# Attention probabilities left undivided: the outputs are multiplied by turned inverse sums

## The chip, the cores and the metric

The kernel runs on one core of a Trainium2 chip, as one launch. The metric is the device time of a launch in microseconds, smaller is better; it comes as the median of several runs, with their extremes. A profile is one more execution, recorded by the hardware profiler.

## The reference

Input x is 64 sequences of 128 tokens with 256 features, the context 64 x 128 x 192. All in float32:

```
lat  = layernorm(x)                          # outer layernorm, then the attention's own with gain
q    = ln(lat) @ Wq.T                        # 4 heads of 64
k, v = [ln(ctx) @ Wkv.T ; ln(lat) @ Wlkv.T]  # 128 context + 128 latent keys
attn = softmax(mask(rmsnorm(q) * 64**-0.5 @ rmsnorm(k).T))
x1   = x + (attn @ v) @ Wo.T + bo
n1   = layernorm(x1)
out  = x1 + routed(n1) + shared(n1)          # 32 experts, 4 a token, in 4 groups of which 2 count;
                                             # and a shared gated FFN of 256
```

The part that matters here is the softmax: exp(s - max) divided by its sum over 256 keys, then multiplied with v.

## The kernel before

There are three stages. The attention stage takes 32 units of two sequences each (j = 0 and 1), one `step(s)` per unit on every engine; the routing of earlier units runs inside the same steps. Then come 288 tiles of the expert FFN, then the shared FFN and the sums. The change touches the attention stage alone.

Each engine runs its own list of instructions in order, written out by hand in its `step`; semaphores tie the lists together. A step s of the attention stage works on several units at once: scores and softmax of s, projections of a = s+1, layernorm turns of s+2, routing of s-2 (cc) and s-3 (r).

TensorE's order in a step (PE `step`, L931): scores j=0 and 1 (L813, with the mask added by L818), turns and logits of routing (L742, L866, L881 to L885), projections of the next unit (L757, L767, L770, again L757), `turn_probs` j=0 (eight 128x128 transposes, L827), `project_v` (L778), `turn_c` (L729), `mix_values` j=0 (sixteen matmuls, L840), `turn_x` (L720), `turn_probs` j=1, `out_proj` j=0 (L852), `turn_k` j=0 (L791, L792), `mix_values` j=1, `turn_k` j=1, `turn_q` (L800), `out_proj` j=1, and then the scores of the next step. Matmuls of 64 rows of the array (L813, L818, L770) or 64 columns (L840) stand between matmuls of all 128 by 128.

ScalarE's order (L1209): rows and layernorms, `exps` j=0 (L1160, which also leaves the sums of the exponentials in den), `weigh_probs` j=0 (L1168: four instructions that multiply the probabilities of a head by its inverse sum), `projected_q` (L1128, L1132), `exps` j=1, the copies of the projections (L1139, L1143, L1145, L1128, L1132), `probs_copy` j=0 (L1175, the turned probabilities from PSUM), the copies of the values (L1152), `weigh_probs` j=1, `o_copy` j=0 (L1182, mixed values from PSUM to oT), `inputs_x` (L1112), `probs_copy` j=1, `inputs_c` (L1120), `k_copy` (L1200), `o_copy` j=1, `k_copy`, `q_copy` (L1206).

VectorE's order (L1648): `maxima` j=0 (L1460), ranks and assignment of routing with the residual (L1473) and statistics (L1402) between, `invert_sums` j=0 (L1466: a reciprocal of 128x4), `maxima` j=1, more routing, `top_scores`, `invert_sums` j=1, two `square_sums` (L1418), `norms` (L1423 to L1448, a chain of small dependent instructions with weights of slots, L1589, between), two `scale_heads` (L1454), slots (L1596), `best_groups` and `best_experts` (L1491 to L1516) with input statistics between, `choose_experts` (L1524 to L1528). In the last step, that of unit 31, `square_sums` and `scale_heads` are gone, and `positions(s-2)` of TensorE stands behind `mix_values` j=1.

GpSimdE issues the scatters of routed rows (L556), each held back by a semaphore of TensorE's progress.

Of the kernel before, what the change touches and what calls it, by code (L numbers as in the profile page):

```python
# [17 lines left out]
P = 128  # L18
NB, D, DC = 64, 256, 192
H, DH = 4, 64  # L20
# [66 lines left out]
def build(nc, x, ctx, mask, gains, w_in_lat, w_in_ctx, wo, bo,  # L87
# [8 lines left out]
    with ExitStack() as c:  # L96
# [45 lines left out]
        probsT = part(2, 2, H * P)  # L142
        oT = part(D)
        vv = part(4 * 2, H, DH)

# [27 lines left out]
        nmax = sb("nmax", [P, 2, H])  # L173
        den, rden = sb("den", [P, 2, H]), sb("rden", [P, 2, H])

# [63 lines left out]
        s_full, m_done, exp_done = sem("s_full"), sem("m_done"), sem("exp_done")  # L239
        den_done, rden_done = sem("den_done"), sem("rden_done")  # L240
        spread = [sem("spread0"), sem("spread1")]
        pt_full, pt_ev = sem("pt_full"), sem("pt_ev")
        pv_full, ot_ev = sem("pv_full"), sem("ot_ev")
        y_full, y_done = sem("y_full"), sem("y_done")
# [465 lines left out]
        def _(pe):  # L710
# [111 lines left out]
            def turn_probs(u, j):  # L822
# [6 lines left out]
                m.then_inc(pt_full, 1)  # L829

            def mix_values(u, j):
                b = 2 * u.n + j
                pe.wait_ge(pt_ev, b + 1)
                pe.wait_ge(pc_free, 2 * u.n + 2)
                ge(pe, ot_ev, b)
                for ch in range(2):
                    for key in range(2):
                        for r in range(2):
                            g, h = 2 * r + ch, 2 * ch + r
                            m = pe.matmul(psO[r * DH:(r + 1) * DH, ch * P:(ch + 1) * P],  # L840
                                          vv[:, 4 * u.par + 2 * j + key, h, :], probsT[:, j, key, g * P:(g + 1) * P],
                                          start=key == 0, stop=key == 1)
                m.then_inc(pv_full, 1)
# [87 lines left out]
            def step(s):  # L931
# [12 lines left out]
                if a.exists():  # L944
                    project_q(a, 0)
                    project_kv(a)
                    project_q(a, 1)
                turn_probs(s, 0)
                if a.exists():
                    project_v(a, 0)  # L950
                    project_v(a, 1)
# [5 lines left out]
                turn_probs(s, 1)  # L957
                out_proj(s, 0)
                if a.exists():
                    turn_k(a, 0)  # L960
# [121 lines left out]
        def _(act):  # L1082
# [72 lines left out]
            def exps(u, j):  # L1155
                b = 2 * u.n + j
                act.wait_ge(m_done, b + 1)
                ge(act, pt_full, b - 1)
                for g in range(H):
                    a = act.activation(probs[:, j, g, :], score_banks[j][:, g // 2, g % 2], ACT.Exp,  # L1160
                                       bias=nmax[:, j, g:g + 1], accum_out=den[:, j, g:g + 1])
                a.then_inc(den_done, 1)

            def weigh_probs(u, j):
                b = 2 * u.n + j
                act.wait_ge(rden_done, b + 1)
                for g in range(H):
                    a = act.activation(probs[:, j, g, :], probs[:, j, g, :], ACT.Copy, scale=rden[:, j, g:g + 1])  # L1168
                a.then_inc(exp_done, 1)
# [7 lines left out]

            def o_copy(u, j):
                b = 2 * u.n + j
                act.wait_ge(pv_full, b + 1)  # L1180
                ge(act, y_full, b)
                act.activation(oT, psO[:, 0:D], ACT.Copy).then_inc(ot_ev, 1)  # L1182

# [25 lines left out]
            def step(s):  # L1209
# [9 lines left out]
                if cc.exists():  # L1219
                    logit_exp(cc)  # L1220
                weigh_probs(s, 0)
                if a.exists():
                    projected_q(a, 0)
                exps(s, 1)
                if a.exists():
                    projected_kv(a, 0)
                    projected_kv(a, 1)
                    projected_q(a, 1)
                probs_copy(s, 0)
                if a.exists():  # L1230
                    values_copy(a, 0)
                    values_copy(a, 1)
                weigh_probs(s, 1)
                o_copy(s, 0)
                if (s + 2).exists():
                    inputs_x(s + 2)
                probs_copy(s, 1)
                if (s + 2).exists():
                    inputs_c(s + 2)
                if a.exists():  # L1240
                    k_copy(a, 0)
                o_copy(s, 1)
                if a.exists():
# [120 lines left out]
        def _(dve):  # L1364
# [98 lines left out]
            def invert_sums(u, j):  # L1463
                b = 2 * u.n + j
                dve.wait_ge(den_done, b + 1)
                dve.reciprocal(rden[:, j, :], den[:, j, :]).then_inc(rden_done, 1)  # L1466

# [180 lines left out]
            def step(s):  # L1648
# [30 lines left out]

                def between_choices(n):  # L1680
                    if ahead.exists() and G_LINKS < n <= G_LINKS + 4:
                        input_part(ahead, n - G_LINKS - 1)
# [8 lines left out]
                invert_sums(s, 0)  # L1691
                maxima(s, 1)
                if r.exists():
                    assign_rest(r, between_moves)
# [7 lines left out]
                if a.exists():  # L1702
                    square_sums(a, 0)
                    square_sums(a, 1)
                norms(run, between_roots if a.exists() else None)
                if a.exists():
                    scale_heads(a, 0)
# [7 lines left out]
                if not cc.exists() or not a.exists():  # L1715
                    residual(s, 0)
                    x1_statistics(s, 0)
                if not cc.exists():
                    if ahead.exists():
                        input_statistics(ahead)  # L1720
# [248 lines left out]
```

## Time and profile before

| | us |
|---|---|
| median of 3 runs | 1344.24 (1341.73 to 1345.44) |
| profiled execution | 1343.46 |
| its span | 1341.5 |
| PE matmul busy | 1298.0 (97%) |
| ScalarE busy | 1011.6 (75%) |
| VectorE busy | 972.0 (72%) |
| GpSimdE busy | 643.4 (48%) |
| L1168, `weigh_probs`, 256 instructions | 109.1, mean 503 ns |

The span is what the instruction records cover; the profiled execution's time is 2 us more, for what lies around it. The attention stage fills the first half of the span, up to about 700 us; its steps repeat with a period of 20.58 us (the load for L813 begins at 319.50 and at 340.08 us).

### The profile page before, as it was taken

What the parts mean: (1) busy time and instruction counts of PE and PEld (TensorE: products, weight loads), DVE (VectorE), ACT (ScalarE), POOL (GpSimd) and SP (SyncE); (2) the same over time, 40 slices, a digit from 0 to 9 for tenths busy, and PEclk for the clock granted to TensorE, in tenths of its full rate; (3) what the DMA queues carried; (4) which work ended last, traced back from release to release, by engine and by line L of the source; (5) the groups of instructions that cost most, each with busy time, mean ns of one, the idle gap of its engine ahead of it and who ended that gap; (6) DMA issues with size and microseconds to landing.
All of it is one profiled execution on the core that took longest, in us unless ns stands there. A gap on an engine that the chain in (4) does not pass through costs nothing.

```text
span 1341.5 us, 32944 instructions
## 1 busy us (share of the span) xinstructions
PE 1298.0 (97%) x8718; PEld 1043.2 (78%) x8718; DVE 972.0 (72%) x4498; ACT 1011.6 (75%) x2730; POOL 643.4 (48%) x724
## 2 busy tenths in 40 slices
PE   6999999999999999999979899999999999999997
PEld 4566676676676766766658799999999999988886
DVE  4578898888988988888887455555555555548887
ACT  4899999999999999999851566766776676653332
POOL 1113555555555555555455366666666666640000
PEclk8999999999999999999989899999999999999999
DMA  8234645535545445454487655555655555438896
GB/s 278 84 133 136 205 162 176 192 131 187 176 138 190 161 153 195 136 179 162 168 304 246 194 169 172 172 172 168 178 169 174 169 173 166 132 114 313 304 319 218
DMA packets 147714, 247.14 MB, mean 184 GB/s; under 512 B 24139, under 2 KB 110413, under 8 KB 146896
## 3 DMA queue, kind: packets, MB, share of 16 engines
q1 hardware_dynamic: 121472, 177.63, 41.3%
q0 software_dynamic: 26064, 67.42, 14.5%
q8 instruction: 77, 1.26, 0.4%
q14 instruction: 101, 0.83, 0.2%
HBM read 104.68 MB, written 119.96 MB: 167 GB/s over the span
## 4 chain that ended last, share of the span: by engine, by line
PE 63%; ACT 21%; DVE 9%; issue 5%; DMA 2%; SPq 0%; POOL 0%; ACTq 0%; DVEq 0%
PE psT L1033 10%; PE ps L1033 9%; PE psS L1043 9%; ACT arena L1168 6%; PE ps L916 6%; PE ps L1024 5%; PE ps L852 4%; ACT arena L1160 4%; PE psS L927 3%; PE psT L827 3%; PE psS L813 3%; PE psO L840 2%; ACT arena L1128 2%; ACT arena L1132 2%; ACT arena L1175 2%
## 5 line engine op out<-in xcount | busy, mean ns | idle before, releaser
L701 POOL DMA_INDIRECT expert_out<-pay,dest x287 | 282.1, 983 | 175.1 <-DVE dest L1878 157.4
L556 POOL DMA_INDIRECT lists<-pay,slot x168 | 174.3, 1037 | 187.7 <-PE psT L827 39.6
L1043 PE MATMUL psS<-arena,history 128*128 x574 | 171.8, 381 | 0.3 <-DVE history L1865 0.3
L1033 PEld LDWEIGHTS ps<-pad,hist_j 128*128 128x128 f32 x1152 | 152.1, 193 | 9.5 <-ACT pad L1315 2.1
L1033 PEld LDWEIGHTS psT<-pad 128*128 128x128 f32 x1144 | 151.0, 192 | 7.3
L1033 PE MATMUL ps<-pad,hist_j 128*128 128x128 f32 x1152 | 152.8, 276 | 1.9 <-ACT pad L1315 1.9
L1033 PE MATMUL psT<-pad 128*128 128x128 f32 x1144 | 151.6, 276 | 0.0
L1872 DVE TENSOR_SCALAR pay<-psS,dest 128x256 f32<-128x256 f32 x287 | 138.9, 484 | 1.6 <-PE psS L1043 1.5
L757 PE MATMUL ps<-arena 128*128 128x512 f32 x256 | 128.3, 624 | 2.6 <-ACT arena L1120 2.0
L556 POOL DMA_INDIRECT lists<-arena,slot x88 | 91.0, 1034 | 79.4 <-PE psT L827 20.6
L1168 ACT ACTIVATE arena<-arena,rden 128x256 f32<-128x256 f32 x256 | 109.1, 503 | 15.2 <-DVE rden L1466 15.1
L1865 DVE TENSOR_TENSOR history<-history,psT 128x128 f32<-128x128 f32 x143 | 41.2, 288 | 102.4 <-ACT history L1326 102.4
L1865 DVE TENSOR_TENSOR history<-history,ps 128x128 f32<-128x128 f32 x144 | 41.5, 288 | 101.2 <-ACT history L1326 101.2
L1024 PE MATMUL ps<-ident,pay 128*128 128x128 f32 x574 | 110.0, 274 | 3.1 <-DMA arena<-in_gate_up 3.0
L1315 ACT ACTIVATE pad<-ps 128x256 f32<-128x256 f32 x287 | 107.7, 375 | 0.0
L1320 ACT ACTIVATE hist_j<-arena 128x512 f32 x144 | 89.6, 622 | 9.4 <-issue 7.6
L1326 ACT ACTIVATE history<-ps 128x128 f32<-128x128 f32 x144 | 39.9, 277 | 70.3 <-PE ps L1033 70.3
L757 PEld LDWEIGHTS ps<-arena 128*128 128x128 f32 x256 | 44.2, 193 | 59.2 <-issue 59.2
L1320 ACT ACTIVATE pad<-arena 128x512 f32 x143 | 88.8, 621 | 0.0
L1326 ACT ACTIVATE history<-psT 128x128 f32<-128x128 f32 x143 | 39.7, 278 | 65.0 <-PE psT L1033 65.0
L1043 PEld LDWEIGHTS psS<-arena,history 128*128 128x128 f32 x574 | 86.9, 192 | 0.7 <-issue 0.7
L1418 DVE TENSOR_REDUCE va<-arena 128x12 f32<-128x768 f32 x64 | 61.0, 953 | 34.2 <-ACT arena L1128 29.1
(238 smaller groups left out, 3284.1 us busy)
## 6 DMA issues: line engine op xcount, KB each, us to landing
lists<-pad SPq DMA_DIRECT2D x72, 516.0 KB, 5.2
pay<-lists SPq DMA_DIRECT2D x287, 129.0 KB, 2.2
arena<-expert_out SPq DMA_DIRECT2D x32, 1024.0 KB, 7.1
pay<-pay SPq DMA_DIRECT2D x42, 384.0 KB, 3.6
x<-in_x SPq DMA_DIRECT2D x32, 256.0 KB, 4.7
out<-arena SPq DMA_DIRECT2D x31, 256.0 KB, 5.8
arena<-arena SPq DMA_DIRECT2D x20, 384.0 KB, 3.4
arena<-in_ctx SPq DMA_DIRECT2D x32, 192.0 KB, 4.6
```

The costliest lines, as they stand in the source:

```text
L556: pool.indirect_dma_start(lists, bass.IndirectOffsetOnAxis(ap=slots(u)[:, j, k:k + 1], axis=0), paid(u)[:, j, k, :], None).then_inc(scat[3 ...
L701: pool.indirect_dma_start(expert_out, bass.IndirectOffsetOnAxis(ap=dest[:, t % DESTS, 1:2], axis=0), yy[n], None, bounds_check=T * TOPK - ...
L757: m = pe.matmul(ps[0][:, :], lnT[:, k, tok], w_lat[:, k, 0:2 * D], start=k == 0, stop=k == 1)
L916: m = pe.matmul(up_banks[u % 2][mm][:, which * D:(which + 1) * D], w[:, k, mm * P:(mm + 1) * P], n1T_of(u)[:, k, :], start=k == 0, stop=k ...
L1024: m = pe.transpose(ps[n % 2][:, k * P:(k + 1) * P], xs[n][:, k * P:(k + 1) * P], ident[:, :])
L1033: m = pe.matmul(ps[2 + n % 2][:, which * P:(which + 1) * P], w_now[1 - n % 2][:, k, which * I:(which + 1) * I], xsT[:, n % 2, k * P:(k + 1 ...
L1043: pe.matmul(dbank[n % 2][:, 0:D], hh[:, n % 4, :], w_dn[:, at(e, 1), :].rearrange("p a n -> p (a n)"), start=True, stop=True)\
L1168: a = act.activation(probs[:, j, g, :], probs[:, j, g, :], ACT.Copy, scale=rden[:, j, g:g + 1])
L1315: act.activation(xsT[:, n % 2, :], ps[n % 2][:, 0:D], ACT.Copy).then_inc(xst_ev, 1)
L1320: act.activation(w_now[1 - n % 2], w_gu[:, at(e, 1)].rearrange("p a k n -> p (a k) n"), ACT.Copy)\
L1865: dve.tensor_tensor(hh[:, n % 4, :], sg[:, n % 4, :], ps[2 + n % 2][:, P:2 * P], ALU.mult)\
L1872: dve.tensor_scalar(yy[n], dbank[n % 2][:, 0:D], dest[:, t % DESTS, 0:1].bitcast(fp32), None, ALU.mult)\
```

## The change

The probabilities stay undivided. `exps` signals `exp_done` itself, and `weigh_probs` is gone. VectorE inverts the four sums of a row as before (into `inv`), and `widen_sums` copies them to 128x256 in the order of the outputs' features (each inverse 64 times). `turn_sums` on TensorE transposes that tile in two 128x128 pieces into the free half of psO; `sums_copy` on ScalarE brings it to SBUF as `wide_sums`. `o_copy` is gone; `divide` on VectorE multiplies psO[0:256] by `wide_sums` into oT. The order of every engine's step changes as the diff shows.

```
+        wide_sums = part(D)
+        rden = part(2, D)
...
 PE
+            def turn_sums(u, j):
+                b = 2 * u.n + j
+                pe.wait_ge(rden_done, b + 1)
+                ge(pe, ot_ev, b)
+                for ch in range(2):
+                    m = pe.transpose(psO[:, D + ch * P:D + (ch + 1) * P], rden[:, j, ch * P:(ch + 1) * P], ident[:, :])
+                m.then_inc(sums_turned, 1)
+
             def mix_values(u, j):
...
-                ge(pe, ot_ev, b)
+                pe.wait_ge(sums_ev, b + 1)
...
                 turn_probs(s, 0)
+                turn_sums(s, 0)
                 if a.exists():
                     project_v(a, 0)
...
                 turn_probs(s, 1)
                 out_proj(s, 0)
+                turn_sums(s, 1)
                 if a.exists():
                     turn_k(a, 0)
                 mix_values(s, 1)
...
 ScalarE
                 ge(act, pt_full, b - 1)
+                ge(act, rden_done, b - 1)
                 for g in range(H):
                     a = act.activation(probs[:, j, g, :], score_banks[j][:, g // 2, g % 2], ACT.Exp,
                                        bias=nmax[:, j, g:g + 1], accum_out=den[:, j, g:g + 1])
-                a.then_inc(den_done, 1)
-
-            def weigh_probs(u, j):
-                b = 2 * u.n + j
-                act.wait_ge(rden_done, b + 1)
-                for g in range(H):
-                    a = act.activation(probs[:, j, g, :], probs[:, j, g, :], ACT.Copy, scale=rden[:, j, g:g + 1])
                 a.then_inc(exp_done, 1)
...
-            def o_copy(u, j):
+            def sums_copy(u, j):
                 b = 2 * u.n + j
-                act.wait_ge(pv_full, b + 1)
-                ge(act, y_full, b)
-                act.activation(oT, psO[:, 0:D], ACT.Copy).then_inc(ot_ev, 1)
+                act.wait_ge(sums_turned, b + 1)
+                ge(act, ot_ev, b)
+                act.activation(wide_sums, psO[:, D:2 * D], ACT.Copy).then_inc(sums_ev, 1)
...
-                weigh_probs(s, 0)
...
                 probs_copy(s, 0)
+                sums_copy(s, 0)
...
-                weigh_probs(s, 1)
-                o_copy(s, 0)
                 if (s + 2).exists():
                     inputs_x(s + 2)
                 probs_copy(s, 1)
+                sums_copy(s, 1)
...
-                o_copy(s, 1)
...
 VectorE
             def invert_sums(u, j):
                 b = 2 * u.n + j
-                dve.wait_ge(den_done, b + 1)
-                dve.reciprocal(rden[:, j, :], den[:, j, :]).then_inc(rden_done, 1)
+                dve.wait_ge(exp_done, b + 1)
+                ge(dve, sums_turned, b - 1)
+                dve.reciprocal(inv[:, j, :], den[:, j, :]).then_inc(inv_done, 1)
+
+            def widen_sums(u, j):
+                dve.wait_ge(inv_done, 2 * u.n + j + 1)
+                dve.tensor_copy(rden[:, j, :].rearrange("p (c r d) -> p c r d", c=2, r=2),
+                                inv[:, j, :].rearrange("p (r c o) -> p c r o", c=2, o=1).to_broadcast([P, 2, 2, DH]))\
+                   .then_inc(rden_done, 1)
+
+            def divide(u, j):
+                b = 2 * u.n + j
+                dve.wait_ge(pv_full, b + 1)
+                dve.wait_ge(sums_ev, b + 1)
+                ge(dve, y_full, b)
+                dve.tensor_tensor(oT, psO[:, 0:D], wide_sums, ALU.mult).then_inc(ot_ev, 1)
...
                 def between_choices(n):
+                    if n == G_LINKS + 1:
+                        divide(s, 1)
...
                 maxima(s, 1)
+                widen_sums(s, 0)
...
                     square_sums(a, 1)
+                widen_sums(s, 1)
                 norms(run, between_roots if a.exists() else None)
+                divide(s, 0)
...
                 if not cc.exists():
+                    divide(s, 1)
```

## Rows read from the trace of the kernel before

**Rows 1.** Stretches: us, each engine's busy us (instructions), TensorE clock, DMA share, GB/s.

```profile
300.00:400.00 100.00, 99.37 (x668) 67.48 (x665) 89.26 (x509) 96.70 (x265) 54.45 (x63) 1.00 0.50 169
```

**Rows 2.** Waits of TensorE's weight loads from 100 to 600 us: total us, times, longest.

```profile
PEld psT L827 <- ACT arena L1168: 8.8, 24, 0.4
```

**Rows 3.** Timeline of one unit's step, weight loads: start, us, line, tile, [idle before].

```profile
326.15 0.19 PEld L767 LDWEIGHTS ps<-arena 128*128 128x128 f32 x1 [0.24 <-issue]
...
327.10 0.30 PEld L770 LDWEIGHTS ps<-arena 64*128 64x128 f32 x4 [0.76 <-issue]
...
334.02 0.42 PEld L720 LDWEIGHTS ps<-ident,arena 128*128 128x128 f32 x4 [0.17 <-issue]
...
334.81 0.86 PEld L827 LDWEIGHTS psT<-ident,arena 128*128 128x128 f32 x8 [0.36 <-ACT arena L1168]
...
337.13 0.85 PEld L840 LDWEIGHTS psO<-arena 128*64 128x64 f32 x16 [0.17 <-ACT arena L1175]
...
339.00 0.73 PEld L852 LDWEIGHTS ps<-arena 128*128 128x128 f32 x4
...
340.08 0.73 PEld L813 LDWEIGHTS psS<-arena 64*128 64x128 f32 x8 [0.35 <-ACT arena L1206]
```

**Rows 4.** The same step, matmuls.

```profile
336.93 0.27 PE L792 MATMUL ps<-ident,arena 128*128 128x128 f32 x1
...
339.11 1.03 PE L852 MATMUL ps<-arena 128*128 128x256 f32 x4
```

**Rows 5.** The same step, ScalarE.

```profile
334.66 0.37 ACT L1182 ACTIVATE arena<-psO 128x256 f32<-128x256 f32 x1
...
335.94 1.02 ACT L1175 ACTIVATE arena<-psT 128x1024 f32<-128x1024 f32 x1
...
339.35 0.68 ACT L1206 ACTIVATE arena<-ps,gain 128x512 f32<-128x512 f32 x1
```

**Rows 6.** The same step, VectorE.

```profile
331.26 0.95 DVE L1418 TENSOR_REDUCE va<-arena 128x12 f32<-128x768 f32 x1 [0.90 <-ACT arena L1128]
...
334.79 0.16 DVE L1448 SCALAR_TENSOR_TENSOR nb<-mv,ra 128x6 f32<-128x6 f32 x1
...
338.29 0.29 DVE L1506 TENSOR_TENSOR t<-sfc,gm 128x32 f32<-128x32 f32 x2
...
341.37 1.22 DVE L1460 TENSOR_REDUCE nmax<-psS 128x4 f32<-128x1024 f32 x1 [0.53 <-PE psS L818]
```

**Rows 7.** VectorE's groups, 100 to 600 us: busy us, mean ns of one, idle before.

```profile
L1473 DVE TENSOR_TENSOR x<-x,ps 128x256 f32<-128x256 f32 x48 | 19.9, 414 | 0.0
...
L1573 DVE COPY history<-given 128x32 f32<-128x32 f32 x25 | 4.3, 174 | 0.0
```

**Rows 8.** One line's instructions, L1596: ns min/median/max.

```profile
L1596 DVE TENSOR_SCALAR slot<-c x32: 162/165/399, 110.2 to 721.3; 128x8 int32<-128x8 f32 x32
```

**Rows 9.** Weight loads in the second unit's step.

```profile
65.18 0.85 PEld L840 LDWEIGHTS psO<-arena 128*64 128x64 f32 x16 [0.54 <-ACT arena L1175]
...
67.30 0.86 PEld L827 LDWEIGHTS psT<-ident,arena 128*128 128x128 f32 x8 [0.68 <-ACT arena L1168]
```

**Rows 10.** Steps of the last two units: matmuls, then VectorE.

```profile
664.22 1.09 PE L827 MATMUL psT<-ident,arena 128*128 128x128 f32 x8 [1.04 <-ACT arena L1168]
...
673.32 0.66 PE L742 MATMUL ps<-ident,pay 128*128 128x128 f32 x4 [2.59 <-ACT pay L1099]
...
685.05 1.09 PE L840 MATMUL psO<-arena 128*64 128x128 f32 x16 [1.11 <-ACT arena L1175]
...
684.55 0.17 DVE L1491 TENSOR_TENSOR gs<-g 128x8 f32<-128x8 f32 x1
...
687.36 0.18 DVE L1528 TENSOR_TENSOR before<-before,chosen 128x32 bf16<-128x32 bf16 x1
...
690.23 0.22 DVE L1538 TENSOR_TENSOR later<-psT,kept 128x64 f32<-128x64 f32 x1 [0.70 <-PE psT L885]
```

**Rows 11.** Chain of waits from 645 to 725 us: start, us, what.

```profile
665.59 6.50 DMA lists<-pay,slot
```

More of the change, by code:

```diff
@@ L173, in build @@
         nmax = sb("nmax", [P, 2, H])
-        den, rden = sb("den", [P, 2, H]), sb("rden", [P, 2, H])
+        den, inv = sb("den", [P, 2, H]), sb("inv", [P, 2, H])
         esc = sb("esc", [P, 2, E])
@@ L239, in build @@
         s_full, m_done, exp_done = sem("s_full"), sem("m_done"), sem("exp_done")
-        den_done, rden_done = sem("den_done"), sem("rden_done")
+        inv_done, rden_done = sem("inv_done"), sem("rden_done")
         spread = [sem("spread0"), sem("spread1")]
         pt_full, pt_ev = sem("pt_full"), sem("pt_ev")
+        sums_turned, sums_ev = sem("sums_turned"), sem("sums_ev")
         pv_full, ot_ev = sem("pv_full"), sem("ot_ev")
```

## The prediction, made before the changed kernel had run

> **What bounds the kernel now.** I read four views. First the timeline by stretches: in the attention stage TensorE has a matmul in flight 99% of the time, ScalarE is busy 97%, VectorE 89% [rows 1]. All three look full, so shares decide nothing; what counts is which engine waits within a step. ScalarE carries the most visible cost of the change, L1168, 109 us over the kernel, and a reader could expect much of it back. Second, the waits: the only place where TensorE plainly waits for it is `turn_probs` j=1, 8.8 us in 24 steps, 0.37 a step [rows 2]. Third, the timeline of one step, instruction by instruction. Its period is 20.58 us (340.08 less 319.50). Apart from the 0.36 before L827 the weight loads follow each other at the matmuls' own pace, with gaps where the array changes its shape [rows 3].
>
> The one gap that has to be judged is the 0.35 before L813, which the profile puts down to ScalarE's `q_copy` (339.35 + 0.68 = 340.03, load at 340.08) [rows 3, 5]. I read it as a gap that stays. When the shape changes, the load waits until the matmul before has streamed: after L767 (0.43 a matmul) load to load is 327.10 - 326.15 = 0.95, that is 0.43 until that matmul starts, 0.43 of streaming and 0.09; after L792 (0.11 a matmul) it is 337.13 - 336.93 = 0.20, so 0.11 and 0.09 [rows 3, 4]. For L852 (0.215 each) the last of four starts at 339.11 + 0.65 = 339.76, and 0.215 + 0.09 behind it is 340.06. ScalarE costs 0.02 there, not 0.35. The Trainium skill has this as a rule ("TensorEngine Tiling (Array Packing)", Key Properties: changing the tiling mode drains the engine); the rows agree. By the rule 0.02 can be won at this place, by the profile's label 0.35.
>
> So TensorE sets the pace, and it has 0.38 us a step to give back.
>
> **The change, part by part, for a steady step.**
>
> *Removed from ScalarE:* eight instructions of L1168 a unit, 3.4 us, and the wait for the reciprocal. Two `o_copy` (0.37) are replaced by two `sums_copy` of the same size, read from the same bank: 0.37 each [rows 5]. ScalarE gets 4 us of air in 20.58. TensorE gets from that only the 0.36 before `turn_probs` j=1 and the 0.02. What is late next is TensorE itself.
>
> *Added to TensorE:* two `turn_sums` of two transposes. Eight such take 0.86 [rows 3], 0.107 each, so 0.43 a step, and nothing hides them, since they stand in the list of the engine that sets the pace. They change no shape, so they add no gap.
>
> *A new wait, `mix_values` j=1 for `sums_copy`.* Between `turn_sums` j=1 and `mix_values` j=1 only `turn_k` j=0 lies. From the start of the last transpose of the sums TensorE is ready for L840 after four more of 0.11 and the gap of 0.20, 0.63 in all. The sums need 0.27 until the transpose ends (L792's duration), 0.04 to ScalarE, 0.37 for the copy and 0.06 back: 0.74 [rows 3 to 5]. A stall of 0.11 to 0.12. ScalarE is free just then: `probs_copy` j=1 (1.02, started at 335.94 when `turn_probs` had ended) ends at about 336.9, with the transposes of the sums. Behind `sums_copy` j=1 are queued `inputs_c` and `k_copy`, for which `turn_k` j=1 and `turn_q` wait; I add 0.03. For j=0 `project_v` (eight matmuls of L852's pace, 1.7 us) covers the copy. Bounds of the new wait: 0 (ScalarE a little quicker) and 0.25 (`sums_copy` behind a late `probs_copy`).
>
> *VectorE.* Each `divide` is L1473's form, a 128x256 multiply with one input in PSUM: 0.41 long, 0.33 to the next instruction [rows 7]. `widen_sums`, a float32 copy of 256 columns, has no row. From below: the 32-column copy, 0.174 long [rows 7], 0.09 to the next. From above: L1473's 0.33, and 0.23 more for a stretch as L1596 once had (162 to 399 ns) [rows 8], 0.56. I take 0.33, its nearest row in size. VectorE gains 2 x 0.33 + 2 x 0.33 = 1.3 us of work a step, against waits of 0.90 before the second L1418 and 0.53 before L1460 [rows 6], and about 0.4 before the second reciprocal. Of the 0.90 ScalarE gives back about 0.4 (then `project_q` j=1 on TensorE is last); `widen_sums` j=1 takes 0.33 of it, and `norms` ends some 0.1 earlier, where it ended at 334.95. `divide` j=0 then runs from about 334.9 to 335.3, and `out_proj` j=0 is due on TensorE at 335.5 (L827 at 334.81 less 0.36, plus 0.21 and 0.82). `divide` j=1 follows L1506, which slips from 338.29 to about 338.5, and ends near 339.1; `out_proj` j=1 is due at 339.2. Both arrive in time, by 0.1 to 0.2 only. L1460 of the next step is met too: two thirds of a microsecond more work since `norms` against a wait of 0.53 and a later TensorE. So VectorE's additions cost nothing as long as this cover is there; if it goes they cost one for one.
>
> Sum of a steady step: 0.43 - 0.36 - 0.02 + 0.12 + 0.03 = +0.20. For 27 steps (units 3 to 29): +5.4 us.
>
> **The ends of the stage.** In the second unit's step TensorE waited longer: 0.68 before L827, and 0.54 where 0.17 is the gap before L840 [rows 9, 3]. 1.05 goes, 0.6 comes, and `projected_q` comes earlier too. For the first three units together -1.0 (0 to -1.8).
>
> In unit 30's step the wait before L827 is 1.04 and goes, against 0.21 of `turn_sums`: -0.83. From there the chain runs over a scatter of 6.50 us to a TensorE that idles 2.59 at 673.32 [rows 10, 11]. The transfer shares the queues with loads that don't come earlier, so I take -0.5 (0 to -0.83).
>
> In unit 31's step VectorE loses its cover. `divide` j=0 stands ahead of `best_groups` of unit 29, in VectorE's list, and must wait for `mix_values` j=0. That began at 685.05 and now comes 0.3 later (behind `sums_copy`): ends 686.4, divided at 686.8. L1491, which started at 684.55, starts 2.2 us later. From it to the end of L1528 are 3.0 us [rows 10]; halfway `divide` j=1 waits in turn for `mix_values` j=1, which ended shortly before 690 (L1538, behind it and `positions`, began at 690.23) and now at 690.2. With 0.33 and the 1.6 us behind it, L1528 is over at 692.1. `positions` of unit 29, then `out_proj` j=1, wait for that on TensorE. `residual` and statistics of j=0, formerly done in a wait, now take 0.7 ahead of L1538, which begins near 692.8: +2.6. The chain of waits runs through that instruction, so it carries on to the expert stage. Range +1 to +4: TensorE's new idle stretch of 2 us could bring its clock down as that of 2.59 did, or part of it is taken up by the waits that follow.
>
> The expert and shared stages are untouched.
>
> **The sum.** 5.4 - 1.0 - 0.5 + 2.6 = +6.5 us on the profiled execution's 1343.5 (span 1341.5): 1350.0. The median of the runs was 0.8 above the profiled one: 1350.8.
>
> **Rivals.**
>
> *A, TensorE was not the bound, and the kernel gets faster.* The place is L813: the label there says ScalarE, and ScalarE was 97% busy. If the 0.35 is a real wait, TensorE gets back 0.36 + 0.35 against 0.43 and 0.15: -0.13 a step, -3.5 over 27; with the ends +1.1, -2.4 (1342); with the new stall absent too (-0.28 a step), -6.5: 1338. It turns faster than before from 0.58 us given back a step. Against it stands the arithmetic of the gaps, to 0.02. Chance 0.12.
>
> *B, VectorE becomes the bound.* If `widen_sums` takes 0.56 and not 0.33, or `norms` doesn't start earlier, both divides are late and `out_proj` waits: 0.3 to 0.5 more a step, 8 to 13 us: 1359 to 1364, middle 1361. For it: VectorE is at 89% and gets 6% more, and the margins are 0.1 to 0.2. Against: 1.8 us of waits. Chance 0.13. The Trainium skill gives a reason for such a stretch ("SBUF — State Buffer", "SBUF: two separate sides"): a float32 SBUF copy on VectorE and GpSimdE exclude each other from a shared pair of ports, and GpSimdE's descriptors for scatters wait as well. By that rule, taken whole, a copy could wait for most of a scatter's issue, near B's upper end. The trace agrees only in part: L1596, a single-source instruction, had a median of 165 ns and once 399 [rows 8].
>
> *C, it comes out even.* The stall before `mix_values` is covered (+0.05 a step, 1.4) and the end costs 1 to 1.5 rather than 2.1 (the delay sinks into waits further on): +1.5, 1346. For it: the stall is a difference of two nearly equal paths. Chance 0.25.
>
> The forecast keeps 0.50; its own range is 1347 to 1355.
>
> **How the numbers follow.** About 0.3%, 4 us, is what a measurement of this kernel can tell from no change: 1340.2 to 1348.3 counts as the same. Faster: half of A and a little of C, 0.08. Same: the rest of A, most of C and the lower edge of the forecast, 0.29. Slower: the remainder, 0.63. The range leaves out the fastest form of A and the upper half of B: 1342 to 1359.
>
> **What would show it.** Right: the period of a step 20.75 to 20.80; no wait before L827; a short wait before L840 (j=1) for `sums_copy`; the 0.35 before L813 still there, though ScalarE now idles for several us a step; VectorE waiting in unit 31's step for both products of `mix_values`, TensorE for `positions`. Wrong: a period below 20.58, with the gap before L813 gone (A); waits of L852 for the divides (B); `widen_sums` outside 0.2 to 0.4.

## The result, and the profile after

| | time us | ratio to before |
|---|---|---|
| before, beside it | 1342.99 median of 4 (1341.18 to 1345.44) | |
| after | 1354.63 median of 4 (1352.76 to 1355.71) | 1.0084, 95% interval [1.0061, 1.0107] |
| after once more, in a later series (j1) | 1358.78 median of 4 (1357.52 to 1359.87) | 1.0112, [1.0091, 1.0132] |

By the medians the change costs 12 us in the first series and 15 in the second (before beside that one: 1343.80). The profiled execution of the first series took 1353.69 (span 1351.6, before 1341.5: +10.1).

The same stretch as in [rows 1] (us, busy of PE, PEld, DVE, ACT, POOL, granted clock, DMA share, GB/s):

```profile
300.00:400.00 100.00, 99.30 (x663) 68.13 (x661) 92.08 (x521) 81.98 (x223) 54.67 (x63) 1.00 0.51 170
```

ScalarE has lost 15 points of busy time, VectorE has gained 3, and TensorE stands where it stood. The weight loads of one step, which answer to [rows 3] (start, us, line, tile; in brackets the gap ahead and what ended it):

```profile
334.17 0.25 PEld L839 LDWEIGHTS psO<-ident,arena 128*128 128x128 f32 x2
334.39 1.60 PEld L781 LDWEIGHTS ps<-arena 128*128 128x128 f32 x8
...
336.65 0.85 PEld L851 LDWEIGHTS psO<-arena 128*64 128x64 f32 x16 [0.17 <-issue]
337.67 0.42 PEld L723 LDWEIGHTS ps<-ident,arena 128*128 128x128 f32 x4 [0.17 <-issue]
338.06 0.90 PEld L830 LDWEIGHTS psT<-ident,arena 128*128 128x128 f32 x8
338.93 0.73 PEld L863 LDWEIGHTS ps<-arena 128*128 128x128 f32 x4
339.69 0.35 PEld L839 LDWEIGHTS psO<-ident,arena 128*128 128x128 f32 x2
...
340.82 0.88 PEld L851 LDWEIGHTS psO<-arena 128*64 128x64 f32 x16 [0.34 <-issue]
...
342.75 0.73 PEld L863 LDWEIGHTS ps<-arena 128*128 128x128 f32 x4
343.81 0.73 PEld L816 LDWEIGHTS psS<-arena 64*128 64x128 f32 x8 [0.33 <-ACT arena L1213]
```

`turn_probs` j=1 (now L830, at 338.06) no longer waits; before, 0.36 stood there. Two pairs of L839 are in the list. The gap before `mix_values` j=1 (L851) is 0.34 where it was 0.17. The gap before the scores (L816) is what it was, 0.33, although ScalarE now stands idle for several us a step. What fills the 0.34 is seen on TensorE and ScalarE, matmuls first:

```profile
339.91 0.38 PE L839 MATMUL psO<-ident,arena 128*128 128x128 f32 x2
```

```profile
339.28 1.02 ACT L1182 ACTIVATE arena<-psT 128x1024 f32<-128x1024 f32 x1
340.32 0.38 ACT L1189 ACTIVATE arena<-psO 128x256 f32<-128x256 f32 x1
340.61 1.15 ACT L1133 ACTIVATE arena<-ps,gain 128x128 f32<-128x128 f32 x3
```

The turning of the sums (`turn_sums` j=1) ends at 339.91 + 0.38 = 340.29, `probs_copy` (L1182) at 340.30, `sums_copy` (L1189) starts at 340.32, and the mix loads 0.12 after its end. VectorE's additions (groups from 100 to 650 us: busy us, mean ns of one, idle before):

```profile
L1485 DVE TENSOR_TENSOR arena<-psO,arena 128x256 f32<-128x256 f32 x52 | 21.8, 420 | 1.1 <-DVE nb L1453 0.2
L1476 DVE COPY arena<-inv 128x256 f32<-128x256 f32 x53 | 15.0, 283 | 0.0
```

The difference of the two executions, cut at TensorE's loads for the scores of units 0, 3, 30 and 31 and at the last instruction of its kind as the last in [rows 10] (the counting of the last unit, 715.32 before, 725.79 after):

| part | forecast | measured |
|---|---|---|
| up to the first scores (31.07, 31.53) | 0 | +0.46 |
| first three periods (61.95, 60.98) | -1.0 | -0.97 |
| 27 steady periods (20.58, 20.88) | +5.4 | +8.1 |
| steps with a late scatter (1.9 after, 0.2 before) | 0 | +1.7 |
| unit 30's step (20.58, 20.62) | -0.5 | +0.04 |
| scores of unit 31 to the last counting (45.83, 46.92) | +2.6 | +1.1 |
| the rest (626.2, 625.8) | 0 | -0.4 |
| sum | +6.5 | +10.1 |

The +1.1 in the step of unit 31 hides a change of TensorE's clock. Before, after an idle stretch of 2.59 us, the granted clock was at half (the lower of its two levels, 1.2 GHz) for some 6 us, and the eight matmuls of the second scores took 2.08. In this execution of the changed kernel it stayed at full (2.4 GHz) after 1.98 us of idling, and the same eight took 1.13. Matmuls before and after, then a stretch of 6 us of each (the clock stands behind the five engines, 0.54 and 1.00):

```profile
674.06 2.08 PE L813 MATMUL psT<-arena 64*128 64x256 f32 x8
```

```profile
682.10 0.66 PE L745 MATMUL ps<-ident,pay 128*128 128x128 f32 x4 [1.98 <-ACT pay L1112]
...
682.82 1.13 PE L816 MATMUL psT<-arena 64*128 64x256 f32 x8
```

```profile
673.50:679.50 6.00, 6.00 (x32) 4.79 (x32) 5.05 (x27) 3.69 (x13) 0.97 (x1) 0.54 0.85 307
682.90:688.90 6.00, 6.00 (x39) 5.16 (x40) 5.65 (x30) 4.37 (x18) 1.95 (x3) 1.00 0.96 318
```

`mix_values` j=0 begins 12.10 behind the unit's scores (678.87), where before it was 15.57 (669.49). So the table compares this step at two clocks; the second execution (j1) shows it at the lower one.

### The profile page after: what moved, and what is told of

The parts are those of the page before. It is cut to its first block, busy times and chain, and to the rows that moved or that the text cites. A ratio compares the mean times of both kernels' runs of the same rounds, so it can differ in the third digit from the quotient of the medians.

```text
span 1351.6 us, 33234 instructions
## 1 busy us (share of the span) xinstructions
PE 1304.5 (97%) x8846; PEld 1056.9 (78%) x8846; DVE 1003.1 (74%) x4626; ACT 920.9 (68%) x2474; POOL 650.4 (48%) x724
## 3 DMA queue, kind: packets, MB, share of 16 engines
q8 instruction: 78, 1.28, 0.4%
## 4 chain that ended last, share of the span: by engine, by line
PE 92%; DMA 3%; DVE 2%; issue 1%; ACT 1%; SPq 0%; POOL 0%; DVEq 0%; ACTq 0%
PE psT L1046 9%; PE ps L1046 9%; PE psS L1056 9%; PE ps L760 9%; PE ps L927 6%; PE ps L1037 5%; PE psO L851 5%; PE ps L770 4%; PE ps L781 4%; PE psS L938 4%; PE ps L863 3%; PE ps L773 3%; PE psT L816 2%; PE psS L816 2%; PE ps L877 2%; PE psT L830 2%
## 5 line engine op out<-in xcount | busy, mean ns | idle before, releaser
L559 POOL DMA_INDIRECT lists<-pay,slot x168 | 178.6, 1063 | 187.1 <-PE psS L830 32.7
L549 POOL TENSOR_TENSOR x<-x,bo_b 128x512 f32<-128x512 f32 x32 | 40.6, 1269 | 92.4 <-PE psS L821 92.4
```

What stands on the lines that cost most here:

```text
L559: pool.indirect_dma_start(lists, bass.IndirectOffsetOnAxis(ap=slots(u)[:, j, k:k + 1], axis=0), paid(u)[:, j, k, :], None).then_inc(scat[3 ...
```

## The experiments

What was left open: whether the steady +0.30 is made of the terms of the forecast, whether ScalarE or VectorE binds instead, and what the late scatters are. "Period" is the time from scores to scores in the steady steps; apart from a few longer steps it repeats to 0.01. e1 to e4 and i1 ran once each (beside e1 to e4 the kernel before took 1341.72), so their periods carry the argument and not their times.

**e1_no_turns.** The changed kernel without the transposes of the sums; `sums_copy` still runs and waits for `widen_sums` instead. (The first transposes of the kernel, outside the steps, also write all of psO here.)

```diff
             def turn_sums(u, j):
-                pe.wait_ge(rden_done, b + 1)
-                ...
-                m.then_inc(sums_turned, 1)
+                return
...
-                act.wait_ge(sums_turned, b + 1)
+                act.wait_ge(rden_done, b + 1)
```

> The changed kernel with turn_sums emptied: the transposes of the sums are left out, so the outputs are scaled by what lies in that half of psO, and sums_copy waits for widen_sums instead. All of VectorE's and ScalarE's new work stays. Period of a steady step (scores to scores) in the changed kernel: 20.88 us, of the kernel before: 20.58. Theory T (TensorE sets the pace; its 0.43 of transposes and the 0.17 stall before mix_values j=1 are paid in full): 20.88 - 0.43 - 0.17 = 20.28, at most 20.33, so below the kernel before. Rival V (the added work of VectorE or its ports sets the pace): 20.8 to 20.9. The time: theory T 28 steps x 0.6 = 17 us under the changed kernel, about 1338; rival V about 1354.

1342.68; period 20.63, not 20.3: between the two theories. Of the 0.60 expected (0.43 of turns, 0.17 of stall) 0.25 came back. Waits of TensorE's weight loads, 100 to 600 us:

```profile
PEld psO L847 <- ACT arena L1178: 9.8, 23, 0.4
...
PEld ps L859 <- DVE arena L1480: 0.8, 3, 0.3
```

`mix_values` j=1 (L847) now waits 0.42. The queue on ScalarE ends just as late: `probs_copy` starts at 335.59 behind `inputs_x`, `sums_copy` at 336.50, the mix loads at 337.00. In pieces: scores to mix j=0 is 0.22 shorter (13.50 against 13.72), mix to mix 0.13 (4.04 against 4.17), and from there to the scores 0.10 longer, because `out_proj` j=1 loads 0.10 late (339.02), behind a `divide` that ends at 338.97. So the turns do cost TensorE what was counted, and right behind them stand ScalarE (0.25 at the mix, beside its drain of 0.17) and VectorE (0.10): 0.22 + 0.13 - 0.10 is the 0.25 that came back.

**e2_no_weigh.** The kernel before without `weigh_probs` (the output is not divided by the sums).

```diff
-                weigh_probs(s, 0)
...
-                weigh_probs(s, 1)
```

> The kernel before with weigh_probs left out and nothing put in its place (the outputs stay undivided): the removal alone. It tells what ScalarE's 3.4 us a step were worth. Theory T: only the wait before turn_probs j=1 (0.36) and 0.02 go, the gap of 0.35 before the scores' first load stays at 0.33 though ScalarE idles for 3 us a step: period 20.20. Rival A (ScalarE was the bound, the gap before the scores is a true wait): the gap falls to 0.1 or less and the period to 19.9. Time by T about 1332, by A about 1324.

1331.95; period 20.26. The wait before `turn_probs` j=1 is gone, the drain before the mix and the gap before the scores stay:

```profile
331.40 0.90 PEld L827 LDWEIGHTS psT<-ident,arena 128*128 128x128 f32 x8
...
333.77 0.85 PEld L840 LDWEIGHTS psO<-arena 128*64 128x64 f32 x16 [0.17 <-ACT arena L1169]
...
336.74 0.73 PEld L813 LDWEIGHTS psS<-arena 64*128 64x128 f32 x8 [0.33 <-ACT arena L1200]
```

ScalarE does 3.4 us less a step, and TensorE gains 0.32: the wait before `turn_probs` j=1, and nothing at the place of rival A. By itself this doesn't settle rival A, since here too `q_copy` ends 0.07 before the load (336.67 and 336.74): it hangs on `turn_q`, which TensorE makes just before. g3 settles it, below.

**e3_idle_turns.** The kernel before with two unused transposes at each of the two places where the changed kernel turns its sums.

```diff
+            def idle_turns():
+                for ch in range(2):
+                    pe.transpose(psO[:, D + ch * P:D + (ch + 1) * P], ident[:, :], ident[:, :])
```

> The kernel before plus transposes of ident into the free half of psO, two behind turn_probs j=0 and two behind out_proj j=0 (results unused): TensorE's added work alone, with no wait attached to it. Theory T: the first pair is swallowed by the 0.36 wait before turn_probs j=1 (it falls to 0.15), the second is paid: period 20.58 + 0.21 = 20.79. Rival V (TensorE has air, the loss comes from VectorE or from the waits): 20.58.

1355.79; period 21.02, +0.44. The wait of 0.36 did not absorb the first pair, since it moved along:

```profile
341.51 0.85 PEld L827 LDWEIGHTS psT<-ident,arena 128*128 128x128 f32 x8 [0.36 <-ACT arena L1174]
```

ScalarE's `weigh_probs` j=1 stands behind `values_copy`, which follows `project_v` on TensorE, and the first pair stands ahead of `project_v`.

**e4_narrow_copy.** The changed kernel with a widening copy of 4 columns in place of 256 (the other columns keep ones).

```diff
-                dve.tensor_copy(rden[:, j, :]...to_broadcast([P, 2, 2, DH]))
+                dve.tensor_copy(rden[:, j, 0:H], inv[:, j, :]).then_inc(rden_done, 1)
```

> The changed kernel with widen_sums copying 4 columns and not 256 (the rest of the tile holds ones, so the outputs are wrongly scaled): the cost of the wide copy alone. It saves VectorE 2 x 0.1 to 0.2 us a step. Theory T: period 20.88 as in the changed kernel, within 0.02. Rival V: 20.88 less 0.2 to 0.3. Rival P (the wide float32 copy holds up GpSimdE's scatters through the shared ports, and so makes the five late scatters for which ScalarE's rows waited in the changed kernel's profile, 1.9 us in all): those waits are gone and GpSimdE's scatter instructions are back from 1063 to 1047 ns mean; by T they don't depend on the copy and come in some executions and not in others.

1360.0; period 20.88 as in the changed kernel. The widening costs TensorE nothing. Its late-scatter steps (21.86, 21.82, 21.78, 21.55) are still there, so the widening copy is not needed for them: rival P falls. In unit 31's step TensorE's clock fell as before the change (0.55 from 685 to 691 us).

**h1_turn_x_first.** The changed kernel, `turn_x` of the unit after next ahead of `mix_values` j=0.

```diff
+                if (s + 2).exists():
+                    turn_x(s + 2)
                 mix_values(s, 0)
-                if (s + 2).exists():
-                    turn_x(s + 2)
```

> The changed kernel with TensorE's turn_x(s+2) moved ahead of mix_values(s,0) (same work, other order). Theory S: the 0.17 us that mix_values(s,1) loses in the changed kernel is ScalarE's queue of inputs_x (1.02), probs_copy j=1 (1.02), sums_copy j=1 (0.38), which starts with the end of turn_x. Starting inputs_x some 1 us sooner takes it off the way: the period goes from 20.88 to about 20.71, 27 steps make 4.6 us, the time is about 1350. Rival W: the stall belongs to the turned sums themselves (they follow out_proj j=0 by 0.76 and end 0.3 before the mix), and stays: period 20.88, 1354.6.

1354.32, ratio 1.0069 [1.0048, 1.0090]; period 20.88, the gap before the mix still 0.34. Theory S falls. `inputs_x` did go out of the way (ScalarE idles 1.03 before `probs_copy`), and `sums_copy` still began only at 340.23, with the mix 0.50 later.

**i1_half_copy.** The changed kernel with `sums_copy` of 128 columns.

```diff
-                act.activation(wide_sums, psO[:, D:2 * D], ACT.Copy)
+                act.activation(wide_sums[:, 0:P], psO[:, D:D + P], ACT.Copy)
```

> The changed kernel in which ScalarE's sums_copy evicts only the first 128 of the 256 turned columns (VectorE multiplies both halves by them, so heads get each other's sums); TensorE does the same work. Theory C: the 0.17 us beyond the drain ahead of mix_values j=1 is the chain end of turn_probs j=1 -> probs_copy j=1 (1.02) -> sums_copy j=1 (0.38) -> mix. A sums_copy shorter by about 0.1 us takes that much off: period 20.78, 27 steps make 2.7 us. Rival W: the stall comes from writing psO again after the turned sums, whatever reads them: period 20.88.

1348.86 in one run; period 20.78, the gap before the mix 0.23. The mix waits for `sums_copy`: one shorter by 0.11 shortens the gap by as much. What `sums_copy` waits for this run leaves open; f2 tells.

**f2_turn_early_end.** The changed kernel, `turn_sums` j=1 ahead of `out_proj` j=0, and the last unit's divides later in VectorE's list.

```diff
-                out_proj(s, 0)
                 turn_sums(s, 1)
+                out_proj(s, 0)
```

> The changed kernel with turn_sums(s,1) ahead of out_proj(s,0), and in the last unit VectorE's divides put to the ninth link of the choice of groups (j=0) and behind choose_experts (j=1). Steady steps: theory C (sums_copy j=1 stands behind probs_copy j=1 on ScalarE, so an earlier turning frees nothing) gives a period of 20.88 as before the move; rival W (the turned sums' own place) 20.71. Last unit: what my prediction counted as 2.6 us of blocking falls to under 1: the counting of the last ranks (VectorE, read_ranks of unit 31) starts about 2 us sooner after the start of that unit's scores than the changed kernel's 21.2 us; the time is 1352 to 1353.

1347.03, ratio 1.0035 [1.0022, 1.0048]; period 20.75, between the two expectations. TensorE and then ScalarE:

```profile
335.63 0.25 PEld L839 LDWEIGHTS psO<-ident,arena 128*128 128x128 f32 x2
335.85 0.73 PEld L863 LDWEIGHTS ps<-arena 128*128 128x128 f32 x4
...
337.39 0.88 PEld L851 LDWEIGHTS psO<-arena 128*64 128x64 f32 x16 [0.20 <-issue]
```

```profile
335.98 1.02 ACT L1182 ACTIVATE arena<-psT 128x1024 f32<-128x1024 f32 x1
336.89 0.39 ACT L1189 ACTIVATE arena<-psO 128x256 f32<-128x256 f32 x1
```

Sums turned early, `sums_copy` follows `probs_copy` by 0.91 instead of 1.04, and of the 0.17 only 0.03 is left. So in the changed kernel the end of `turn_sums` j=1 releases it, and 0.13 behind stands `probs_copy`. In the last unit the counting did not begin 2 us sooner, as expected, but 1.3 (45.60 from the unit's scores instead of 46.92). That pair is again at two clocks: in f2 the clock fell to half in this step, in the changed kernel's first execution not. Against h1 and i1, where it fell at the start of the step as in f2, f2 is 2.4 sooner (48.04 in both); part of this is a second fall of the clock, which f2 doesn't have.

**g1_values_later.** The kernel before, `values_copy` of j=1 behind `weigh_probs` j=1.

```diff
-                    values_copy(a, 1)
                 weigh_probs(s, 1)
+                if a.exists():
+                    values_copy(a, 1)
```

> The kernel before, with ScalarE's values_copy(a,1) (0.39 us) moved behind weigh_probs(s,1). Question: what is the 0.36 us wait before turn_probs j=1 worth by itself? Rival N (what my prediction counted with): weigh_probs starts 0.27 sooner, the wait shrinks to 0.09, and the period falls by that 0.27, from 20.58 to 20.31, time about 1335.5. Theory S: behind that wait stands the same queue of ScalarE (weigh 1.69, o_copy 0.37, inputs_x 1.02, probs_copy 1.02), whose length the move doesn't change, and mix_values j=1 waits for its end: most of the 0.27 comes back as a wait there, the period is 20.50 to 20.56, the time 1341 to 1343.

1339.47, ratio 0.9973 [0.9957, 0.9989]; period 20.45, half of the 0.27 that the wait gave up:

```profile
333.54 0.85 PEld L827 LDWEIGHTS psT<-ident,arena 128*128 128x128 f32 x8
...
335.91 0.85 PEld L840 LDWEIGHTS psO<-arena 128*64 128x64 f32 x16 [0.21 <-ACT arena L1175]
```

**g2_o_on_dve, g3_both, g4_one_on_dve.** The kernel before with `o_copy` on VectorE, where the changed kernel has its divides: both of a step (g2); both, with the order of g1 (g3); only j=0, with the order of g1 (g4). In unit 31's step their places differ from the changed kernel's.

```diff
+            def o_copy(u, j):
+                b = 2 * u.n + j
+                dve.wait_ge(pv_full, b + 1)
+                ge(dve, y_full, b)
+                dve.tensor_copy(oT, psO[:, 0:D]).then_inc(ot_ev, 1)
```

> The kernel before, with o_copy (two 0.37 to 0.41 us evictions a step) on VectorE instead of ScalarE, at the places where the changed kernel has its divides. Theory S: the wait before turn_probs j=1 stays 0.36 (weigh_probs starts when it did), the mix stays behind its drain of 0.17, the period stays within 0.05 of 20.58 and the time within 2 us of 1343. Rival V (VectorE bounds): its own work grows by 0.6 to 0.8 us a step, maxima and reciprocals come later, the period grows to 20.8 or more, 1349 or more.

> The kernel before with both moves: values_copy(a,1) behind weigh_probs(s,1), and o_copy on VectorE. Theory S: now ScalarE's queue ahead of probs_copy j=1 is shorter by o_copy's 0.27 as well, and nothing takes the place of the wait that shrinks: the period is about 20.31, 27 steps times 0.27 are 7 us, the time about 1335.5. Rival V: VectorE's added work comes back as later maxima: 1343 or more. Rival N (the wait alone counts): as g1_values_later, with no gain over it.

> The kernel before, with values_copy(a,1) behind weigh_probs(s,1), and only the first o_copy of a step on VectorE (the second stays on ScalarE, where g3_both waited 0.46 for VectorE). Theory S: ScalarE's queue ahead of mix_values j=1 is shorter by 0.27 than in g1_values_later, the 0.04 left of its wait goes, out_proj j=0 waits at most 0.1 for VectorE: period 20.40 to 20.50, time 1338 to 1340.5, no clear difference to g1_values_later (20.45). Rival V: VectorE can't take even one: the scaling of the heads comes later and with it turn_k, period 20.6 or more.

| | time us | ratio | period |
|---|---|---|---|
| g2 | 1351.62 | 1.0058 [1.0038, 1.0077] | 20.89 |
| g3 | 1350.95 | 1.0047 [1.0033, 1.0062] | 20.87 |
| g4 | 1335.54 | 0.9949 [0.9934, 0.9963] | 20.41 |

The expectations for g2 and g3 missed the mechanism: the times came out near rival V's, but not by late maxima. They are in time, and the second eviction isn't. In g3, weight load and VectorE's copy ahead of it:

```profile
344.74 0.73 PEld L852 LDWEIGHTS ps<-arena 128*128 128x128 f32 x4 [0.46 <-DVE arena L1465]
```

```profile
344.27 0.42 DVE L1465 COPY arena<-psO 128x256 f32<-128x256 f32 x1
```

This run also settles the gap before the scores. With `out_proj` j=1 late, `q_copy` (ScalarE) is over at 344.61 + 0.68 = 345.29, half a microsecond ahead of the load of the next scores, and the gap is 0.33 all the same, now without ScalarE's label:

```profile
344.61 0.68 ACT L1200 ACTIVATE arena<-ps,gain 128x512 f32<-128x512 f32 x1
```

```profile
345.80 0.73 PEld L813 LDWEIGHTS psS<-arena 64*128 64x128 f32 x8 [0.33 <-issue]
```

With that one back on ScalarE (g4) the drains are left (the gaps where the array changes its shape), and some 0.08 each before `turn_probs` j=1 and `out_proj` j=0; it is the fastest kernel that computes the reference.

**j1_after_again.** The changed kernel, not edited.

> The changed kernel once more, unchanged: does the excess of 1.9 us that its profile shows beside the steady period (four steps of 21.01 to 21.67 us, in which turn_n1 waits for ScalarE's rows_to_scatter and that for a scatter that lands late) belong to the kernel or to the execution? Theory X (execution): a new execution has these waits in other steps, fewer or none; the steady period is 20.88 again. Rival K (kernel): four waits in the same steps (those that start at 239, 344, 469 and 575 us), of the same size.

1358.78, ratio 1.0112 [1.0091, 1.0132]; period 20.88. The long steps are the same four, begun at 238, 344, 470 and 575 us, and longer: 21.86, 21.83, 21.86, 21.86, in sum 3.9 us against 1.9 in the first execution. The same four appear in e4. In the steps beside them nothing waits; in these ScalarE stands before `rows_to_scatter`:

```profile
239.14 1.09 ACT L1112 ACTIVATE pay<-x,nb,ra 128x256 f32<-128x256 f32 x2 [1.08 <-DMA lists<-pay,slot]
```

So the places belong to the kernel, the size to the execution; but h1, which differs by one moved operation, has none (1354.32, though), f2 has one of 0.41 and one of 0.09, e1 three (the longest 0.26), g4 three (the longest 0.66), and the kernel before has two, of 0.08 and 0.09.

The profiled execution is 5.6 us longer than the first (1357.2 against 1351.6). Besides 2.0 in the late steps, 4.0 of it lie in unit 31's step and behind it (scores to the last counting 50.92 instead of 46.92). Here TensorE idled 2.96 before `turn_n1`, and the clock was at half behind it:

```profile
685.80:691.80 6.00, 6.00 (x24) 4.76 (x24) 5.64 (x30) 4.19 (x18) 0.97 (x1) 0.50 1.07 361
```

`mix_values` j=0 begins 17.41 behind the scores (15.57 before, 12.10 in the first execution), and VectorE waits for both products:

```profile
698.93 0.42 DVE L1485 TENSOR_TENSOR arena<-psO,arena 128x256 f32<-128x256 f32 x1 [2.13 <-PE psO L851]
...
702.64 0.42 DVE L1485 TENSOR_TENSOR arena<-psO,arena 128x256 f32<-128x256 f32 x1 [2.00 <-PE psO L851]
```

## Why the prediction was right, and where it was off

The mechanism of the steady step is right; its size and the ends are off. The forecast's own range was 1347 to 1355: the first series lies at its upper edge (1354.63), the second beyond it (1358.78), inside the wide range that ends at 1359 and next to rival B's 1359 to 1364, though nothing of B happened. That the first series came so near is in part luck: 2.7 us of stall and turns, 1.7 of late scatters and 0.5 in unit 30's step were missed, and about 3 us of clock in unit 31's step paid some of it back.

*What binds.* Right. TensorE's own list sets the pace: adding 0.43 to it cost 0.44 (e3), and taking the turns out gave back 0.25, up to where the next engine stood (e1). That g2 and g3, where VectorE is late, have nearly the same period as the changed kernel (20.89, 20.87, 20.88) is chance: f2 gives VectorE the same work in the steady steps and has 20.75.

*The gap before the scores.* Right, and shown: 0.33 with ScalarE relieved (after, e2), 0.33 in g3 where `q_copy` had ended 0.50 before, in all kernels 0.33 to 0.36. Rival A falls. In e2 ScalarE lost 3.4 us a step and TensorE gained 0.32, which is the wait before `turn_probs` j=1.

*The wait that goes, the turns that come.* Right: -0.36 and +0.43.

*The new stall before the mix.* The mechanism is as forecast: `turn_sums` j=1, then `sums_copy`, then the mix, with only `turn_k` to cover it (i1, f2). The size was 0.17 instead of 0.12, within the bounds given. Of the path of 0.74 that the forecast added up, the way back from the copy to the load was mis-sized: 0.12 (340.70 to 340.82) and not 0.06. Between the runs I had taken it for ScalarE's queue (theory S of h1, C of f2), and each was off by the part that the prediction had right.

*The steady step.* +0.30 instead of +0.20, and a period of 20.88 where 20.75 to 20.80 was to be seen: this is the term that was mis-sized, 2.7 us over 27 steps. 0.05 is the stall and 0.03 the mix itself, slower to load behind it; the 0.03 for queued copies came, at `turn_q`, which starts 0.12 behind the end of `k_copy`. The remaining 0.02 lies in no single gap.

*The ends.* The first three units: right (-0.97). Unit 30: the wait before `turn_probs` went (1.28 in the weight loads). But the forecast set only one pair of turns against it, 0.21, and left out the second pair and the stall of 0.17 before the mix. A wait came besides that it did not have: `out_proj` j=0 stood behind a `divide`.

```profile
673.97 0.73 PEld L863 LDWEIGHTS ps<-arena 128*128 128x128 f32 x4 [0.45 <-DVE arena L1485]
```

Unit 31: in the first execution the blocking is the one described for j=1 only. `divide` j=0 finds its product ready (it starts at 693.90 with no wait; `mix_values` j=0 began at 690.97), and TensorE's `out_proj` j=0 waits for it; then VectorE waits 1.81 for the second product and TensorE 2.03 for `positions` (matmuls, then VectorE):

```profile
694.38 1.13 PE L863 MATMUL ps<-arena 128*128 128x256 f32 x4 [1.29 <-DVE arena L1485]
696.29 1.09 PE L851 MATMUL psO<-arena 128*64 128x128 f32 x16 [0.56 <-ACT arena L1189]
699.42 0.18 PE L892 MATMUL psT<-chosen,tri 128*128 128x32 bf16 x1 [2.03 <-DVE before L1544]
```

```profile
697.42 0.42 DVE L1485 TENSOR_TENSOR arena<-psO,arena 128x256 f32<-128x256 f32 x1 [1.81 <-PE psO L851]
...
700.03 0.21 DVE L1557 TENSOR_TENSOR later<-psT,kept 128x64 f32<-128x64 f32 x1
```

And it cost 1.1 and not 2.6: the counting at 700.03 (L1557, the L1538 of before) is 21.16 behind the unit's scores, before it was 20.74. The step that failed is "now comes 0.3 later" for `mix_values` j=0. It came 3.5 sooner against the scores: 0.6 by a shorter wait at `turn_n1` (1.98 for 2.59), and about 3 because the clock did not fall. The forecast had thought of a new fall of the clock, not that the old one could go. In e4, where it fell as before, `mix_values` j=0 begins at 15.44 (before 15.57), VectorE waits for both products (1.73 and 2.00), the counting is 22.94 behind the scores, 2.2 later than before, and the last one 2.9 later (48.69 and 45.83): near the forecast's 2.6, though e4 spares VectorE a little work. In j1 the clock was low for longer, and it cost 5.1.

*VectorE.* In the steady steps it stayed in time, with a little more room than the forecast's 0.1 to 0.2: `divide` j=1 ends at 342.46 (342.05 + 0.41) for a load at 342.75. `widen_sums` took 0.28, and 0.20 to the next instruction where 0.33 was counted. Rival B did not happen, yet it was near: with the turns taken out of TensorE's list (e1) it costs 0.10, and in g2 and g3, where VectorE makes both evictions of the kernel before, 0.30 and 0.46.

*Not in the prediction:* the late scatters, 1.9 us here and 3.9 in the second execution. What makes a scatter land late in these four steps stays open. The widening copy is not the cause (e4). Rival C (1346) had the end's size in the first execution (1 to 1.5), but for another reason, and no stall.

## What to carry to other kernels

Work that an engine with slack gives up is worth only the waits that the bounding engine has for it, here 0.36 of 3.4 us a step (e2: 0.32); any repayment on the bounding engine is paid in full. To find how far a shorter queue helps, look for the second chain that ends just behind the first: in e1, f2 and g1 it stood 0.1 to 0.3 us behind. A step of the stage's end is to be compared at the same granted clock, or a few us of it pass for a gain or a loss of the change. The better use of the same observation was to reorder ScalarE's list and to move one eviction, not two, to VectorE (g4, 0.5% faster than before).

## What the runs showed of the hardware

*A scatter's issue waits for VectorE.* GpSimdE's issue of a scatter takes 0.97 us, or much longer when it starts during the second half of `scale_heads`, a two-operand float32 multiply in SBUF; in the steady steps it is mostly the sixth scatter of a step. In the changed kernel, VectorE and then GpSimdE:

```profile
255.01 1.82 DVE L1459 TENSOR_TENSOR arena<-arena,ra 128x768 f32<-128x768 f32 x2
```

```profile
253.14 0.96 POOL L559 DMA_INDIRECT lists<-pay,slot  x1 [0.99 <-PE ps L781]
255.95 1.70 POOL L559 DMA_INDIRECT lists<-pay,slot  x1 [1.85 <-PE psT L830]
```

It ends 0.82 after the multiply. In three other kernels the same holds: before, multiply to 254.49 and issue 253.86 to 255.33 (1.47), 0.84; g1 1.75 long, 0.83; e2 1.38, 0.84. In h1 the issue starts at 234.96, just ahead of the second multiply, and takes 0.97. That is as if the issue's own work started only when the multiply had ended. The Trainium skill has an exclusive lock on a port pair that the two engines share ("SBUF — State Buffer", "SBUF: two separate sides"): a VectorE instruction with two SBUF inputs takes it, against a GpSimdE instruction that reads SBUF. The trace agrees, if the issue counts as one that reads SBUF (its `slot`); no run here tells which of its accesses waits. The 399 ns of L1596 in [rows 8] are at 696.80, beside a scatter's issue from 696.26 to 697.23. The steady period is not longer for it: g1 has the longest issues and a shorter period. Whether it has a part in the late scatters is open: h1, the changed kernel without late steps, has no such issue from unit 4 to unit 29, while g1 has them and no step longer by more than 0.1.

*The clock at the stage's end.* Behind the wait before `turn_n1` in unit 31's step the granted clock fell to half in the kernel before (2.59 us of idling) and in j1 (2.96), and it stayed at full in the changed kernel's first execution (1.98). In g4 it fell after 1.97 (0.60 from 667.5 to 671.5). So the length of that wait alone does not tell it.

*A widening copy is quick.* 128x256 float32 with a broadcast source took 0.283, less than the 0.41 of a copy of that size out of PSUM (L1465 of g3).
